# Token attention: queries and keys from one projection of 128 columns, parts put in place by transfers inside SBUF

## The chip, the cores and the metric

One core of a Trainium2 chip runs the whole program. The metric is device time in microseconds; before the change the median of three runs is 577.97 us (576.04 to 580.85).

## The reference, cut to what matters

The input is x, four images of 128 channels and 32 x 32 pixels. A convolution attention is added to it, then a token attention, then a mixture of eight experts of which each token takes two. The change touches the token attention alone, for each image with 1024 tokens of 128 channels:

```python
def _L1_attn_ref(inputs, W_q, W_k, W_v, W_o, b_o):
    Q = jnp.einsum('bsd,du->bsu', inputs, W_q)
    K = jnp.einsum('bsd,du->bsu', inputs, W_k)
    V = jnp.einsum('bsd,du->bsu', inputs, W_v)
    attn = jnp.einsum('bqu,bku->bqk', Q, K) * scale
    w = jax.nn.softmax(attn, axis=-1)
    out = jnp.einsum('bqk,bku->bqu', w, V)
    return jnp.einsum('bsu,ud->bsd', out, W_o) + b_o + inputs
```

Here d is 128 and u is 64; inputs are the tokens after a layer norm.

## The kernel before

The attention part is a run of eight phases: convolution phases of images 0, 1 and 2, token phase of image 0, convolution phase of image 3, token phases of images 1, 2 and 3. Each phase has eight steps, one for each tile of 128 queries. The steps are pipelined: in step g TensorE computes the scores of step g + 1 into one of two score buffers S, transposes the probabilities of step g (L1244), and multiplies those of step g - 1 with the values (L1258, L1264). VectorE takes the row minimum of the (negated) scores (L885) and in convolution phases copies half of the transposed probabilities (L894); ScalarE does the exponentials (L692, L697) and the other copies of probabilities (L706) and outputs (L711).

The preparation of later phases is cut into small units, called fillers, each with a short name, that are spread over three slots in every step. All engines walk the same list: `fill(u, b)` on an engine does that engine's part of unit u of image b. A table of strings sets the order. EARLY normalises an image after its convolution attention and before its token attention, MID projects it for the token attention, POST normalises it afterwards. MID is laid over the first slots of a phase, and EARLY or POST of another image over the same slots, one slot later:

```python
SLOTS_OF_STEP = 3
EARLY = "cs0 - - cs1 - ca0 - ca1 c0 c1 o0 o1 - ts0 - ts1 - ta0 - ta1"
MID = "l0 l1 v0 v1 q0 k0 k1 q1"
POST = "ps0 - - ps1 - pa0 - pa1+pc r0 r1 g0 g1"
```

MID of images 0, 1, 2 and 3 lies in convolution phase 2, convolution phase 3, token phase 1 and token phase 2. In a name, 0 and 1 are the halves of 512 tokens. l transposes the normalised tokens into operandT; v, q and k project values, queries and keys; cs, ps are statistics for a norm (L931, L934, then an inverse square root on GpSimd, L612 and L614); ca, pa apply it (L946); pc copies the normalised tokens to the rows for dispatch (L778). Units with a matmul take the PSUM banks TA and TB by turns, and a unit waits until the one two before it is copied out.

On each engine the three slots of a step stand at fixed places. TensorE: scores, output projection, slot 0, transposes, slot 1, values, slot 2. VectorE: minimum of the next step, normalisation of an output, slot 0, copy of probabilities, slot 1, slot 2. ScalarE: slot 0, copy of probabilities, slot 1, copy of outputs, exponentials of the next step, slot 2.

Scores are computed exactly enough by splitting queries and keys into a rounded part (hi, in the type F32R) and a remainder (lo). QS holds the query's hi in partitions 0 to 63 and its lo in 64 to 127; KH holds the key's hi twice, KL the key's lo twice. Two matmuls, QS with KH and QS with KL, give all four products. Because each tile needs both halves, the weights Wq2 and Wk2 hold W_q and W_k twice, side by side, and a query or key unit projects the same 64 columns into both halves of the partitions. A query unit is one matmul on TensorE (L1358, two passes in the trace), a rounding copy on ScalarE to all of QS (L765) and a subtraction on VectorE for the lower half of QS (L994, 64 partitions); a key unit is L1360, L767 and a subtraction of 128 partitions into KL (L996). VectorE waits for ScalarE's copy (hi_done), and the bank is free only after the subtraction.

QS, KH and KL lie in the tile CQ that the convolution phases also use, in the one of its two buffers that is free at the time. SyncE's queue holds all large transfers in program order: inputs, then for each image the stores and loads that put convolution queries and keys in place (L447 to L463), then the rows of the expert stage.

## Time and profile before

| | us |
|---|---|
| median of three runs | 577.97 |
| lowest and highest | 576.04, 580.85 |
| profiled execution, whole | 577.57 |
| its span in the profile | 575.6 |
| attention part, first scores to the first expert tile | about 33 to 363 |
| expert stage | about 363 to 575 |

The profile is one execution. Its span leaves out about 2 us that the device time includes. Busy times of TensorE are modelled at their ends, since matmuls are pipelined: the time at which the next instruction of the queue starts says more than a duration.

### The profile page before, as it was taken

Reading aid. Unit: us, or ns where it says so; the run is one execution under the profiler, and the core shown is the slowest. Engines: PE = TensorE matmul, PEld = TensorE weight load, DVE = VectorE, ACT = ScalarE, POOL = GpSimd, SP = SyncE. Lnnn points to the kernel's source line nnn. Section 1 sums busy time; section 2 is a strip of 40 time slices with the busy share of each in tenths; the row PEclk is TensorE's granted clock in tenths of the full one; section 3 lists DMA queues with packets and bytes.
Section 4 is the critical chain, followed back from the end, with each engine's and each line's share of the span. In section 5 each row is a group of like instructions: output and inputs, shape, how many; then the busy total and the mean of one; then the engine's idle time right before and its main releaser. Section 6 shows DMA issues by size and latency. Waiting matters only on the chain.

```text
span 575.6 us, 11859 instructions
## 1 busy us (share of the span) xinstructions
PE 476.1 (83%) x3510; PEld 372.4 (65%) x3511; DVE 349.9 (61%) x1023; ACT 304.8 (53%) x794; POOL 182.0 (32%) x199
## 2 busy tenths in 40 slices
PE   3758878788688997898998967788988998998891
PEld 3447666566466766676777756467766876876770
DVE  4633686677855767577976758274783443445461
ACT  2237776677665687666566645335533443443341
POOL 4001001131130230010454443167655773333230
PEclk9959999998999998899899979799999999999896
DMA  8595712500005200000000010112222331226424
GB/s 260 146 229 184 204 27 85 145 1 2 2 1 174 56 1 1 2 2 1 6 29 30 24 34 29 47 47 75 72 66 61 93 100 51 60 60 193 143 96 132
DMA packets 39066, 42.74 MB, mean 74 GB/s; under 512 B 6555, under 2 KB 29556, under 8 KB 39012
## 3 DMA queue, kind: packets, MB, share of 16 engines
q1 hardware_dynamic: 33242, 31.94, 20.3%
q0 software_dynamic: 4608, 9.99, 5.1%
q8 instruction: 29, 0.48, 0.4%
q10 hardware_dynamic: 1162, 0.14, 0.2%
q14 instruction: 25, 0.20, 0.1%
HBM read 24.73 MB, written 17.85 MB: 74 GB/s over the span
## 4 chain that ended last, share of the span: by engine, by line
PE 56%; DVE 14%; ACT 11%; issue 10%; DMA 6%; SPq 1%; POOL 1%; DVEq 0%; POOLq 0%; ACTq 0%
PE S L1409 12%; PE S L1244 8%; PE PO L1425 7%; ACT shared L692 6%; PE TA L1417 3%; PE OM L1258 2%; PE S L1236 2%; PE OM L1264 2%; DVE lowest L885 2%; DMA xs<-slots 2%; PE S L1237 2%; DVE late L946 2%; ACT shared L706 2%; PE TA L1340 2%; PE OM L1401 1%
## 5 line engine op out<-in xcount | busy, mean ns | idle before, releaser
L885 DVE TENSOR_REDUCE lowest<-S 128x4 f32<-128x1024 f32 (+1 forms) x64 | 78.0, 1220 | 57.8 <-PE S L1232 30.2
L1409 PE MATMUL S<-w_T,shared 128*128 x284 | 97.0, 465 | 5.5 <-ACT shared L792 4.4
L602 POOL DMA_INDIRECT y_rows<-shared,xs x71 | 68.2, 960 | 89.8 <-ACT shared L803 81.7
L1244 PE MATMUL S<-ident,shared 128*128 128x128 f32 x512 | 73.2, 290 | 17.1 <-ACT shared L692 15.9
L706 ACT ACTIVATE shared<-S 128x512 f32<-128x512 f32 (+1 forms) x64 | 51.8, 809 | 58.7 <-PE S L1244 58.7
L1166 DVE TENSOR_TENSOR late<-S,shared 128x341 f32<-128x341 f32 x71 | 36.4, 513 | 70.6 <-ACT shared L797 70.4
L1244 PEld LDWEIGHTS S<-ident,shared 128*128 128x128 f32 x512 | 61.1, 148 | 27.6 <-ACT shared L692 21.4
L596 POOL DMA_INDIRECT slots<-rows_both,pos_i x64 | 62.4, 975 | 43.0 <-PE S L1244 23.8
L797 ACT ACTIVATE shared<-S 128x341 f32<-128x341 f32 x71 | 32.3, 455 | 81.2 <-PE S L1409 80.1
L1425 PE MATMUL PO<-w_T,shared 114*128 x426 | 61.6, 281 | 10.2 <-DVE shared L1171 5.6
L1425 PEld LDWEIGHTS PO<-w_T,shared 114*128 114x128 f32 x426 | 53.5, 192 | 24.2 <-issue 17.4
L692 ACT ACTIVATE shared<-S,lowest 128x256 f32<-128x256 f32 x128 | 58.7, 478 | 10.7 <-DVE lowest L885 10.7
L1409 PEld LDWEIGHTS S<-w_T,shared 128*128 128x128 f32 x284 | 49.8, 196 | 22.4 <-issue 9.1
L612 POOL TENSOR_SCALAR rs_v<-mv 128x8 f32<-128x8 f32 x12 | 2.9, 243 | 160.8 <-DVE mv L934 160.8
L1171 DVE COPY shared<-TA 114x384 f32<-114x384 f32 x71 | 39.5, 556 | 17.8 <-PE TA L1417 13.8
L803 ACT ACTIVATE shared<-PO,xs 128x128 f32<-128x128 f32 x71 | 26.1, 367 | 27.0 <-PE PO L1425 26.9
L1232 PE MATMUL S<-CK,CQ 96*128 96x256 f32 x128 | 26.9, 337 | 12.4 <-DMA CQ<-q_pass 6.1
L697 ACT ACTIVATE shared<-S,lowest 128x1024 f32<-128x1024 f32 x32 | 35.5, 1111 | 1.8 <-DVE lowest L885 1.6
L1264 PE MATMUL OM<-shared,Vt 128*64 128x128 f32 x512 | 36.1, 284 | 0.0
L1417 PE MATMUL TA<-ident,late 128*114 128x128 f32 x213 | 35.7, 276 | 0.0
L1236 PE MATMUL S<-CQ 128*128 128x512 f32 x64 | 30.0, 468 | 6.2 <-ACT shared L706 3.1
L1264 PEld LDWEIGHTS OM<-shared,Vt 128*64 128x64 f32 x512 | 28.2, 140 | 8.7 <-issue 8.5
(297 smaller groups left out, 839.2 us busy)
## 6 DMA issues: line engine op xcount, KB each, us to landing
CQ<-q_pass SPq DMA_DIRECT2D x24, 256.0 KB, 5.1
xs<-slots SPq DMA_DIRECT2D x71, 65.0 KB, 1.9
late<-y_rows SPq DMA_DIRECT2D x8, 512.0 KB, 4.8
q_pass<-late SPq DMA_DIRECT2D x6, 512.0 KB, 3.6
x<-in_x SPq DMA_DIRECT2D x4, 512.0 KB, 6.0
out<-x SPq DMA_DIRECT2D x8, 256.0 KB, 2.1
CK<-k_pass SPq DMA_DIRECT2D x12, 128.0 KB, 3.0
rows_both<-in_L_ffn_w SPq DMA_DIRECT2D x1, 1364.0 KB, 9.1
```

Of the source, the lines that this page charges most:

```text
L596: pool.indirect_dma_start(slots, bass.IndirectOffsetOnAxis(pos_i[:, b % 2, j % 2, j // 2:j // 2 + 1], 0), rows[j % 2][:, (b % 2) * NT + j ...
L602: pool.indirect_dma_start(y_rows, bass.IndirectOffsetOnAxis(xs[:, k, C:C + 1].bitcast(I32), 0), ys[:, k % NC, :], None).then_inc(ys_out[k] ...
L692: ins = act.activation(probs[:, g % 2, h * KEYS:(h + 1) * KEYS], S[g % 2][:, h * KEYS:(h + 1) * KEYS], ACT.Exp, bias=lowest[:, g % 2, h:h ...
L706: act.activation(probsT[:, g % 2, at:HW], S[g % 2][:, at:HW], ACT.Copy).then_inc(s["ptB_copied"], 1)
L885: nc.vector.tensor_reduce(lowest[:, g % 2, 0:n], S[g % 2][:, :].rearrange("p (h k) -> p h k", h=n), AX.X, ALU.min).then_inc(s["low_ready"], 1)
L1171: nc.vector.tensor_copy(hidT[0:HC, k % NC, :], TA[0:HC, 0:CHUNKS * P]).then_inc(s["hT_dve"], 1)
L1236: mm(dst, QS[T][:, tile(j)], KH[T][:, r], start=True, stop=False)
L1244: last = tr(S[g % 2][:, tile(k)], probs[:, g % 2, tile(k)], ident[:, :])
L1264: last = mm(out_[r, :], Vt[:, b % 2, kt, :], pT[:, tile(kt)], start=(kt < 2), stop=(kt >= NT - 2))
L1409: last = mm(S[k % 2][:, m * 512:m * 512 + H], xsT[:, k % NC, :], w13_T[:, bass.ds(e, 1), m * H:(m + 1) * H].rearrange("p a h -> p (a h)"), ...
L1417: last = tr(TA[0:HC, tile(c)], hid[:, k % NC, c * HC:(c + 1) * HC], ident[:, :])
L1425: last = mm(PO[:, 0:P], hidT[0:HC, k % NC, tile(c)], w2_T[0:HC, bass.ds(e, 1), tile(c)].rearrange("p a c -> p (a c)"), start=(c == 0), sto ...
```

## The change

The weights of queries and keys stand side by side in one tile Wqk, of which the query half is scaled. One unit, m, projects both for half of the tokens: partitions 0 to 63 get queries, 64 to 127 keys. ScalarE's rounding copy writes to QS, so that QS has the query's hi above and the key's hi below; VectorE's subtraction writes both remainders to KL. A new function of SyncE, move_qk, then puts the parts in place by transfers from one part of SBUF to another, with a wait between them: the key's hi from the lower half of QS to both halves of KH; the query's lo from the upper half of KL to the lower half of QS; the key's lo from the lower half of KL to its upper half. The first scores of a token phase wait for all three. MID has six units instead of eight, with m0 and m1 ahead of the values.

```diff
-MID = "l0 l1 v0 v1 q0 k0 k1 q1"
+MID = "l0 l1 m0 m1 v0 v1"
...
-            for dst, w in ((Wq2, "L1_attn_W_q"), (Wk2, "L1_attn_W_k"), (Wv2, "L1_attn_W_v")):
-                for k in range(2):
-                    sp.dma_start(dst[:, k * U:(k + 1) * U], a[w]).then_inc(s["small_in"], 16)
+            for dst, k, w in ((Wqk, 0, "L1_attn_W_q"), (Wqk, 1, "L1_attn_W_k"), (Wv2, 0, "L1_attn_W_v"), (Wv2, 1, "L1_attn_W_v")):
+                sp.dma_start(dst[:, k * U:(k + 1) * U], a[w]).then_inc(s["small_in"], 16)
...
+            def move_qk(b):
+
+                T = TOK_SET[b]
+                wait_copied(sp, ("m0", b), ("m1", b))
+                for k in range(2):
+                    sp.dma_start(KH[T][k * U:(k + 1) * U, :].bitcast(F32), QS[T][U:P, :].bitcast(F32)).then_inc(s["k_moved"], 16)
+                sp.wait_ge(s["k_moved"], 32 * (b + 1))
+                sp.dma_start(QS[T][U:P, :].bitcast(F32), KL[T][0:U, :].bitcast(F32)).then_inc(s["q_moved"], 16)
+                sp.wait_ge(s["q_moved"], 16 * (b + 1))
+                sp.dma_start(KL[T][0:U, :].bitcast(F32), KL[T][U:P, :].bitcast(F32)).then_inc(s["kl_moved"], 16)
...
                 stack_q(b, 1)
+                if b == 2:
+                    move_qk(0)
+            for b in range(1, B):
+                move_qk(b)
...
-                elif u in ("q0", "q1"):
+                elif u in ("m0", "m1"):
                     act.activation(QS[T][:, r], bank[:, :], ACT.Copy).then_inc(s["hi_done"], 1)
-                elif u in ("k0", "k1"):
-                    act.activation(KH[T][:, r], bank[:, :], ACT.Copy).then_inc(s["hi_done"], 1)
...
-                elif u in ("q0", "q1"):
-                    copied(V.tensor_tensor(QS[T][U:P, r], bank[U:P, :], QS[T][U:P, r].bitcast(F32), ALU.subtract))
-                elif u in ("k0", "k1"):
-                    copied(V.tensor_tensor(KL[T][:, r], bank[:, :], KH[T][:, r].bitcast(F32), ALU.subtract))
+                elif u in ("m0", "m1"):
+                    copied(V.tensor_tensor(KL[T][:, r], bank[:, :], QS[T][:, r].bitcast(F32), ALU.subtract))
...
+                    if kind == "tok":
+                        pe.wait_ge(s["k_moved"], 32 * (b + 1))
+                        pe.wait_ge(s["q_moved"], 16 * (b + 1))
+                        pe.wait_ge(s["kl_moved"], 16 * (b + 1))
...
-                elif u in ("q0", "q1"):
+                elif u in ("m0", "m1"):
                     pe.wait_ge(s["wq_scaled"], 1)
-                    last = mm(bank[:, :], Wq2[:, :], operandT[:, r], start=True, stop=True)
-                elif u in ("k0", "k1"):
-                    last = mm(bank[:, :], Wk2[:, :], operandT[:, r], start=True, stop=True)
+                    last = mm(bank[:, :], Wqk[:, :], operandT[:, r], start=True, stop=True)
```

VectorE in the first three steps of convolution phase 2, before, where image 0 is projected. CQ is the tile that holds QS, KH and KL, late the normalised tokens of image 1, shared the transposed probabilities, TA and TB the PSUM banks:

```order
L934 BN_AGGR mv<-stats 128x2 x4
L885 TENSOR_REDUCE lowest<-S 128x4
...
L894 COPY shared<-S 128x512
L994 TENSOR_TENSOR CQ<-TA,CQ 64x512
L931 BN_STATS stats<-late 128x6 x4
L934 BN_AGGR mv<-stats 128x2 x4
L996 TENSOR_TENSOR CQ<-TB,CQ 128x512
L885 TENSOR_REDUCE lowest<-S 128x4
...
L996 TENSOR_TENSOR CQ<-TA,CQ 128x512
L946 TENSOR_SCALAR late<-late,mv,rs_y 128x128 x4
L894 COPY shared<-S 128x512
L994 TENSOR_TENSOR CQ<-TB,CQ 64x512
```

The same stretch now:

```order
L945 BN_AGGR mv<-stats 128x2 x4
L1005 TENSOR_TENSOR CQ<-TA,CQ 128x512
L896 TENSOR_REDUCE lowest<-S 128x4
...
L1005 TENSOR_TENSOR CQ<-TB,CQ 128x512
L905 COPY shared<-S 128x512
L942 BN_STATS stats<-late 128x6 x4
L945 BN_AGGR mv<-stats 128x2 x4
L896 TENSOR_REDUCE lowest<-S 128x4
...
L957 TENSOR_SCALAR late<-late,mv,rs_y 128x128 x4
L905 COPY shared<-S 128x512
```

Four subtractions have become two, and these stand one step earlier, the first ahead of a row minimum and the second ahead of a copy of probabilities.

TensorE in token phase 1, before, where image 2 is projected, from its first unit after the transposes of the tokens to the third step's values. Wv, Wq and Wk are the weights, ident marks a transpose, Vt the values:

```order
L1363 MATMUL TA<-Wv,operandT 128x128 x4
...
L1363 MATMUL TB<-Wv,operandT 128x128 x4
L1244 MATMUL S<-ident,shared 128x128 x8
L1358 MATMUL TA<-operandT,Wq 128x512
L1264 MATMUL OM<-shared,Vt 64x128 x8
L1360 MATMUL TB<-operandT,Wk 128x512
...
L1275 MATMUL PO<-Wo,outT 128x128
L1360 MATMUL TA<-operandT,Wk 128x512
L1244 MATMUL S<-ident,shared 128x128 x8
L1358 MATMUL TB<-operandT,Wq 128x512
L1264 MATMUL OM<-shared,Vt 64x128 x8
```

The same stretch now:

```order
L1371 MATMUL TA<-operandT,Wqk 128x512
...
L1371 MATMUL TB<-operandT,Wqk 128x512
L1257 MATMUL S<-ident,shared 128x128 x8
L1374 MATMUL TA<-Wv,operandT 128x128 x4
L1277 MATMUL OM<-shared,Vt 64x128 x8
L1374 MATMUL TB<-Wv,operandT 128x128 x4
...
L1288 MATMUL PO<-Wo,outT 128x128
L1257 MATMUL S<-ident,shared 128x128 x8
L1277 MATMUL OM<-shared,Vt 64x128 x8
```

The merged units have taken the places of the value units, the value units those of the first query and key unit, and in the third step transposes and values follow each other without a unit between them.

## Rows read from the trace of the kernel before

**Rows 1.** The page's first part: span, then TensorE's busy time, share and instructions.

```profile
span 575.6 us, 11859 instructions
PE 476.1 (83%) x3510; PEld 372.4 (65%) x3511; DVE 349.9 (61%) x1023; ACT 304.8 (53%) x794; POOL 182.0 (32%) x199
```

**Rows 2.** Groups by line and shape: busy us, mean ns of one, idle before.

```profile
L1358 PE MATMUL TA<-operandT,Wq 128*128 128x512 f32 x8 | 4.1, 594 | 0.0
L994 DVE TENSOR_TENSOR CQ<-TA,CQ 64x512 fp32r<-64x512 f32 x4 | 2.8, 694 | 3.4 <-ACT CQ L765 3.4
L765 ACT ACTIVATE CQ<-TA 128x512 fp32r<-128x512 f32 x4 | 2.4, 594 | 0.5 <-PE TA L1358 0.5
```

**Rows 3.** Order of time, convolution phase 2: start us, us, engine, instruction, idle before.

```profile
126.99 0.40 ACT L769 ACTIVATE Vt<-TA 128x256 f32<-128x256 f32 x1
...
130.65 0.87 DVE L931 BATCH_NORM_STATS2 stats<-late 128x6 f32<-128x128 f32 x4
...
131.55 0.38 DVE L934 BATCH_NORM_AGGREGATE mv<-stats 128x2 f32<-128x6 f32 x4
...
132.44 1.67 POOL L614 TENSOR_TENSOR rs_y<-rs_v,minus_half 128x8 f32<-128x8 f32 x1
...
133.12 1.22 DVE L885 TENSOR_REDUCE lowest<-S 128x4 f32<-128x1024 f32 x1
...
134.66 0.68 DVE L996 TENSOR_TENSOR CQ<-TA,CQ 128x512 fp32r<-128x512 f32 x1
...
135.26 1.11 DVE L946 TENSOR_SCALAR late<-late,mv,rs_y 128x128 f32<-128x128 f32 x4
...
136.28 0.69 DVE L894 COPY shared<-S 128x512 f32<-128x512 f32 x1
...
137.00 0.69 DVE L994 TENSOR_TENSOR CQ<-TB,CQ 64x512 fp32r<-64x512 f32 x1
...
137.02 0.74 PE L1232 MATMUL S<-CK,CQ 96*128 96x256 f32 x4 [2.04 <-DVE shared L894]
...
137.72 1.11 DVE L946 TENSOR_SCALAR late<-late,mv,rs_y 128x128 f32<-128x128 f32 x4
...
138.32 1.91 PE L1244 MATMUL S<-ident,shared 128*128 128x128 f32 x8
...
138.87 1.23 DVE L885 TENSOR_REDUCE lowest<-S 128x4 f32<-128x1024 f32 x1
```

**Rows 4.** Windows: us, PE, PEld, DVE, ACT, POOL busy (instructions), PEclk, DMA, GB/s.

```profile
138.00:143.00 5.00, 5.00 (x38) 4.07 (x36) 3.04 (x8) 2.91 (x9) 0.00 (x0) 0.66 0.00 2
240.00:262.00 22.00, 21.79 (x184) 16.57 (x184) 14.32 (x41) 16.58 (x31) 1.90 (x2) 1.00 0.00 1
```

**Rows 5.** Order of time, convolution phase 3.

```profile
219.39 1.11 DVE L946 TENSOR_SCALAR late<-x,mv,rs_y 128x128 f32<-128x128 f32 x4
...
220.60 2.01 ACT L778 ACTIVATE rows_both<-late 128x1024 f32<-128x1024 f32 x2 [1.79 <-DVE late L946]
```

**Rows 6.** Order of time, token phase 1, third step, TensorE.

```profile
252.32 1.02 PE L1360 MATMUL TA<-operandT,Wk 128*128 128x512 f32 x2
...
253.18 1.04 PE L1244 MATMUL S<-ident,shared 128*128 128x128 f32 x8
...
254.06 1.02 PE L1358 MATMUL TB<-operandT,Wq 128*128 128x512 f32 x2
...
255.01 1.09 PE L1264 MATMUL OM<-shared,Vt 128*64 128x128 f32 x16
```

**Rows 7.** Order of time, token phase 2, ScalarE.

```profile
300.15 2.01 ACT L778 ACTIVATE rows_both<-late 128x1024 f32<-128x1024 f32 x2 [0.64 <-DVE late L946]
```

**Rows 8.** DMA issues (KB each, median us to landing), and image 1's first token scores.

```profile
CQ<-q_pass SPq DMA_DIRECT2D x24, 256.0 KB, 5.1
out<-x SPq DMA_DIRECT2D x8, 256.0 KB, 2.1
...
236.97 0.50 PE L1236 MATMUL S<-CQ 128*128 128x512 f32 x1 [0.21 <-DVE shared L894]
```

More of the change, by code:

```diff
@@ L122 @@
     LAST_UNITS
-BANKED = [f for f in FILLERS if f[0] in "kT0 kT1 qv0 qv1 Q0 Q1 K V c0 c1 o0 o1 l0 l1 q0 q1 k0 k1 v0 v1 r0 r1 g0 g1 wa wb wc rank".split()]
+BANKED = [f for f in FILLERS if f[0] in "kT0 kT1 qv0 qv1 Q0 Q1 K V c0 c1 o0 o1 l0 l1 m0 m1 v0 v1 r0 r1 g0 g1 wa wb wc rank".split()]
 NORMS = [f for f in FILLERS if f[0] in ("cs1", "ts1", "ps1")]
@@ L167, in build @@
         o_wTg = sb("o_wTg", [P, P])
-        Wq2 = sb("Wq2", [P, P])
-        Wk2 = sb("Wk2", [P, P])
+        Wqk = sb("Wqk", [P, P])
         Wv2 = sb("Wv2", [P, P])
@@ L271, in build @@
         OM, PO, TA, TB = (ps(n, [P, 512]) for n in ("OM", "PO", "TA", "TB"))
-        names = """wq_scaled x_in0 x_in wKQV_in w_in const_z const_set pad_z wt_done wt_used bias_done bias_used gn_pe gn_dve gn_read w1_in w3_in
+        names = """k_moved q_moved kl_moved wq_scaled x_in0 x_in wKQV_in w_in const_z const_set pad_z wt_done wt_used bias_done bias_used gn_pe gn_dve gn_read w1_in w3_in
             w2stage_in small_in rows_in dve_pre q_put0 q_put1 k_put q_stacked0 q_stacked1 k_stacked scores_done low_ready exp_done pt_done ptA_copied ptB_copied
@@ L642, in step @@
                 slot(2)
-            pool.wait_ge(s["small_in"], 16 * 8)
-            nc.gpsimd.tensor_scalar(Wq2[:, :], Wq2[:, :], -TOK_SCALE, None, ALU.mult).then_inc(s["wq_scaled"], 1)
+            pool.wait_ge(s["small_in"], 16 * 6)
+            nc.gpsimd.tensor_scalar(Wqk[:, 0:U], Wqk[:, 0:U], -TOK_SCALE, None, ALU.mult).then_inc(s["wq_scaled"], 1)
             pool.wait_ge(s["bias_used"], 3)
@@ L952, in fill @@
                 V = nc.vector
-                if u in ("Q0", "Q1", "K", "q0", "q1", "k0", "k1"):
-                    dve.wait_ge(s["hi_done"], sum(g[0] in ("Q0", "Q1", "K", "q0", "q1", "k0", "k1") for g in FILLERS[:FILLERS.index(f) + 1]))
+                if u in ("Q0", "Q1", "K", "m0", "m1"):
+                    dve.wait_ge(s["hi_done"], sum(g[0] in ("Q0", "Q1", "K", "m0", "m1") for g in FILLERS[:FILLERS.index(f) + 1]))
                 elif u in ("V", "wc", "g0", "g1", "re"):
@@ L1223, in scores @@
                         pe.wait_ge(s["q_stacked0"], 16 * 3 * (b + 1))
-                    wait_copied(pe, *((u, b) for u in (("V",) if kind == "conv" else ("q0", "q1", "k0", "k1", "v0", "v1"))))
+                    wait_copied(pe, *((u, b) for u in (("V",) if kind == "conv" else ("m0", "m1", "v0", "v1"))))
+                    if kind == "tok":
+                        pe.wait_ge(s["k_moved"], 32 * (b + 1))
+                        pe.wait_ge(s["q_moved"], 16 * (b + 1))
+                        pe.wait_ge(s["kl_moved"], 16 * (b + 1))
                 if j == NT // 2 and kind == "conv":
@@ L1319, in fill @@
                 for k, sources in {"Q": ("kT",), "K": ("qv0", "qv1"), "V": ("qv0", "qv1"), "o": ("c",),
-                                   "v": ("l",), "q": ("l",) if u[:2] != "qv" else (), "k": ("l",) if u[:2] != "kT" else (),
+                                   "v": ("l",), "m": ("l",),
                                    "g": ("r",)}.items():
@@ L1392, in _ @@
             pe.wait_ge(s["const_set"], 3)
-            pe.wait_ge(s["small_in"], 16 * 8)
+            pe.wait_ge(s["small_in"], 16 * 6)
             pe.wait_ge(s["bias_used"], 3)
```

## The prediction, made before the change was run

> **What bounds the kernel now.** I read the page's first part, then the groups of instructions by line, then the order of time in the four places where a token image is projected, then the DMA issues. The span of 575.6 us has TensorE busy for 83% of it [rows 1]; VectorE and ScalarE are less busy, but the attention stages are a loop in lockstep (scores, row minimum, exponentials, transposes, copy out, values), so what counts is which engine closes the loop in a given step, and that differs between the places. I call them A (image 0, projected inside convolution phase 2, about 122 to 140 us), B (image 1, inside convolution phase 3, the same pattern 81.67 us later: its last normalisation starts at 219.39 against 137.72 in A [rows 3, 5]), C (image 2, inside token phase 1, about 243 to 259 us) and D (image 3, inside token phase 2, about 284 to 302 us).
>
> The work that the change touches is small: 16 copies on ScalarE and 16 subtractions on VectorE of 0.59 to 0.69 us each, four images times four units, and as many projections on TensorE, each a pair of matmul passes of 594 ns [rows 2], where each row is the share of one bank and one kind. Outside the four places the rows of instructions are unchanged.
>
> In A and B, VectorE closes the loop. In the third step of A it runs without a gap: minimum at 133.12, subtraction of a key half at 134.66, first half of the normalisation at 135.26, and only at 136.28 the copy of the probabilities for which TensorE waits: its next scores start at 137.02 after 2.04 us idle. Then the subtraction of a query half at 137.00, the other half of the normalisation at 137.72, and the next minimum at 138.87, although its scores had been there before [rows 3]. In C and D TensorE closes the loop: in 240 to 262 us it is busy 21.79 of 22.00 us [rows 4], and the last two projections stand squarely in its queue, from 252.32 to 253.18 before the transposes and from 254.06 to 255.01 before the values [rows 6].
>
> **The change part by part.** Two projections of an image go, those in the third step. The first two steps keep as many units as before: the two merged projections stand where the two value projections stood, and these where the first query and the first key projection stood; the second key and the second query projection, in the third step, have no successor. On TensorE that is an even trade: a merged unit fills about 0.86 us (252.32 to 253.18), and the value unit that it changes places with was in the same queue before.
>
> TensorE: per image 2 units, 0.86 + 0.95 = 1.81 us; four images 7.2 us. ScalarE: 2 copies of 0.594 us, 1.2 us per image. VectorE: 2 operations of about 0.69 us (the half-height L994 costs as much as a full one), 1.38 us per image. These don't add up, since they lie beside each other; the place decides which counts.
>
> Place A, replayed from rows 3. The value copy at 126.99 becomes the rounding copy of the first merged unit, 0.60 us, to 127.59. Behind it VectorE subtracts (0.69, to 128.3), and only then takes the minimum of that step. Minimum with what follows it to the next own operation is 133.12 to 134.66, 1.54 us: 129.8. Second subtraction 0.69: 130.5. Probability copy, 136.28 to 137.00, 0.72: 131.2. Four statistics and aggregates, 130.65 to 131.93, 1.28: 132.5, where they ended at 131.93. So the early part of the step is later by 0.5 us, and with it GpSimd's square root: it ended at 132.44 + 1.67 = 134.11 and will end at about 134.6. The minimum at 133.12 now follows the statistics directly, 132.4, and ends with its followers at 133.95. The normalisation therefore starts at 134.6 instead of 135.26, and the probability copy comes about 0.7 us earlier, at 135.6. This is the gain of A: 0.7 us, less than the two subtractions, because the square root is late next. The second half of the normalisation then gains another 0.7 to 0.8, which matters only where something waits for it.
>
> Place B: something does. ScalarE copies the rows of image 0 for dispatch there, 2.01 us at 220.60, and waited 1.79 us for exactly that second half [rows 5]. That start moves by about 1.5 us. Behind it TensorE's values and transposes under the lowered clock move by 0.7 only. Between 0.7 and 1.5 I take 1.1 us.
>
> Place C: transposes start 0.86 us earlier, values 1.81 earlier [rows 6]. VectorE has no probability copy there, so the early subtractions delay nothing that is waited for: the minimum moved behind the first subtraction should still be done before the exponentials that want it, since ScalarE reaches them only after its copies. I take 1.7 us. Place D is C with the row copy of ScalarE at 300.15, which waits for the normalisation [rows 7]; that one moves by the two subtractions and more, so TensorE's 1.81 stands: 1.8 us.
>
> Sum: 0.7 + 1.1 + 1.7 + 1.8 = 5.3 us. Each place gives between nothing (a wait elsewhere takes it up) and about 1.95 us (all of VectorE's 1.38 plus the 0.6 by which its minimum starts earlier).
>
> The new transfers: per image two copies of the key half (64 partitions of 4 KB, 256 KB each, side by side), then one of the query remainder, then one of the key remainder, three hops in series on SyncE's queue. The trace has no transfer inside SBUF. The nearest rows of the same size are 2.1 us (SBUF to memory) and 5.1 us (memory into 32 partitions) to landing [rows 8]; I take the slow one, since few partitions is what they have in common: 3 x 5.1 = 15.3 us. In B the second subtraction ends about 130.5 + 81.7 = 212.2 us and the first scores of image 1 are at 236.97 [rows 8], 24.7 us later, so 9 us are left over; A and C have 25 us and more. Cost: nothing by either end. By the Trainium skill, page "SBUF — State Buffer", section on the DMA port swizzle, a transfer on 64 partitions reaches only half of the SBUF ports; an estimate with its 218 GB/s is 1.2 us of pure movement for 256 KB, so it would not fill the slack either. The trace agrees in kind only: 32 partitions took 5.1 us where 128 took 2.1 us [rows 8], with other sources and more packets.
>
> On SyncE nothing waits behind these hops that is needed soon: after image 0's comes the key store of convolution image 3, tens of microseconds later, and after the rest the token loads, which wait for the routing table. TensorE gets three more semaphore waits at the start of each token phase and two fewer copy waits; I count nothing. Two small weight loads at the start go away, nothing on the path.
>
> **The rivals.** First, a larger gain. In A and B the granted clock falls just after TensorE's wait: 0.66 on average in 138 to 143 us, which is between the two levels of 1.2 and 2.4 GHz, and the eight transposes at 138.32 take 1.91 us [rows 3, 4]. If the shorter step avoids that, up to 5.00 x 0.34 = 1.7 us comes back at each of the two places, and with the full 1.95 elsewhere the gain is 8 to 9.5 us: 568.3 to 570 us. Against it: by the replay TensorE's idle time before the scores of A even grows a little (its last projection is gone), so the low stretch should stay. Chance 0.15.
>
> Second, the gain is taken up. The early subtractions put ScalarE's copy, VectorE's subtraction and the minimum in series in the first step; if the delay of 0.5 us passes through to the exponentials, A and B give nothing and C and D 1 us each: 576 us. For it speaks that in B and D ScalarE carries a 2 us copy at the same spot; against it the 0.86 and 0.95 us blocks in a full TensorE queue. Chance 0.24.
>
> Third, slower through the clock. Less matmul work between waits may lower the clock at places where it is full now. Each new low stretch costs up to the same 1.7 us; it decides from the fourth on: 572.5 + 4 x 1.7 = 579.3 us, 1.3 above the median before. By the Trainium skill, page "TensorE: Matmul & The Clock Gate", Part 1, the chip sets this clock by how busy the array has been lately, so by that rule removing projections can cost what it saves; the trace agrees that the low stretch follows an idle wait (2.04 us [rows 3]) and shows a full clock, 1.00, in 240 to 262 us where the queue is full [rows 4], and it stays nearly full there without the two units. Chance 0.06.
>
> Fourth, slower through the hops. Were a hop longer than 24.7 / 3 = 8.2 us, each token phase would begin late: at 12 us a hop, 36 - 24.7 = 11 us a phase, four times, 45 us less the 5.3, some 617 us. No row comes near. Chance 0.04. The forecast itself holds 0.51.
>
> **How the numbers follow.** The profiled execution took 577.57 us (span 575.6), 0.4 under the median of 577.97 of the runs shown. 577.57 - 5.3 = 572.3; from the median 572.7; I say 572.5. The range: down to 568.2 for the larger gain, up to 577.3 where nearly all is taken up; it leaves out the two slower rivals and the ends. About 1% (5.8 us, 572.2) is what a measurement of this kernel can tell from no change, and the forecast lies just inside: of its 0.51, 0.27 falls beyond 1%. With the larger gain, 0.15, faster by over 1% has 0.42; within 1% has 0.24 + 0.24 + most of the third rival, 0.06 less 0.01: 0.53; slower by over 1% the rest, 0.05.
>
> **What would show it.** Right: in A the probability copy of the third step about 0.7 us earlier relative to the first step, with the normalisation waiting for GpSimd; in C transposes directly behind the output projection and the values 1.8 us earlier; each hop landing in 2 to 5 us, and no wait at the first scores of a token phase. Wrong: a first step longer by over 0.5 us in C or D, a hop above 8.2 us, or the granted clock below 1.00 in 240 to 262 us. The expert stage behind the attention must keep its length; if it does not, the difference there is not of this change.

## The result and the profile after

Over 20 runs of each kernel on the same chips the changed kernel took 572.95 us (median, 566.85 to 579.95) and the kernel before 579.76 us (574.66 to 584.61, and one run of 2524.37). The ratio is 0.988, with a 95% interval of 0.9858 to 0.9903: 6.8 us faster, where 572.5 us in all and a gain of 5.3 us were forecast. A repeat of the changed kernel in another set gave 573.0 against 579.48 us, ratio 0.9894 (0.9858 to 0.9929). Both kernels have single slow runs, over 1.5% above their fastest; the ratios here and below leave these out, so they are not quite the quotients of the medians.

The page's first part, to set beside [rows 1]:

```profile
span 574.0 us, 11821 instructions
...
PE 475.6 (83%) x3494; PEld 375.2 (65%) x3495; DVE 343.0 (60%) x1015; ACT 301.0 (52%) x786; POOL 182.1 (32%) x199
```

VectorE loses 6.9 us and 8 instructions, ScalarE 3.8 us and 8, which is the count of the change. TensorE loses 16 matmuls but only 0.5 us of busy time. These sums tell little: the same eight transposes take 1.04 us at the full granted clock and 1.91 us at the lower level, and most of the low stretches lie elsewhere in every execution. The span of this one execution is only 1.6 us shorter than before, because its attention began 2.65 us later (first copy of probabilities at 42.45 us, before 39.8) and its stages outside the four places ran 3.1 us longer. So I read place by place.

The measure is ScalarE's copy of probabilities, which comes once in each step. From the copy in an image's first projecting step to the copy four steps later, before the change:

```profile
123.98 0.60 ACT L706 ACTIVATE shared<-S 128x512 f32<-128x512 f32 x1 [0.69 <-PE S L1244]
...
146.05 0.60 ACT L706 ACTIVATE shared<-S 128x512 f32<-128x512 f32 x1 [0.18 <-PE S L1244]
...
205.08 0.60 ACT L706 ACTIVATE shared<-S 128x512 f32<-128x512 f32 x1 [0.69 <-PE S L1244]
...
227.23 0.60 ACT L706 ACTIVATE shared<-S 128x512 f32<-128x512 f32 x1 [1.19 <-PE S L1244]
...
243.53 1.02 ACT L706 ACTIVATE shared<-S 128x1024 f32<-128x1024 f32 x1 [0.28 <-PE S L1244]
...
265.03 1.02 ACT L706 ACTIVATE shared<-S 128x1024 f32<-128x1024 f32 x1 [0.18 <-PE S L1244]
...
284.95 1.02 ACT L706 ACTIVATE shared<-S 128x1024 f32<-128x1024 f32 x1 [0.29 <-PE S L1244]
...
306.89 1.02 ACT L706 ACTIVATE shared<-S 128x1024 f32<-128x1024 f32 x1 [1.58 <-PE S L1244]
```

and the same copies after it:

```profile
126.69 0.60 ACT L719 ACTIVATE shared<-S 128x512 f32<-128x512 f32 x1 [0.69 <-PE S L1257]
...
146.37 0.60 ACT L719 ACTIVATE shared<-S 128x512 f32<-128x512 f32 x1 [0.18 <-PE S L1257]
...
206.08 0.60 ACT L719 ACTIVATE shared<-S 128x512 f32<-128x512 f32 x1 [0.69 <-PE S L1257]
...
227.12 0.60 ACT L719 ACTIVATE shared<-S 128x512 f32<-128x512 f32 x1 [1.32 <-PE S L1257]
...
242.21 1.02 ACT L719 ACTIVATE shared<-S 128x1024 f32<-128x1024 f32 x1 [0.28 <-PE S L1257]
...
262.23 1.02 ACT L719 ACTIVATE shared<-S 128x1024 f32<-128x1024 f32 x1 [0.18 <-PE S L1257]
...
282.34 1.02 ACT L719 ACTIVATE shared<-S 128x1024 f32<-128x1024 f32 x1 [0.28 <-PE S L1257]
...
302.23 1.02 ACT L719 ACTIVATE shared<-S 128x1024 f32<-128x1024 f32 x1 [1.58 <-PE S L1257]
```

The differences of each pair are the first two lines of this table; the others are worked out in the same way from the other runs' traces (us):

```
                                   A      B      C      D     sum
before                          22.07  22.15  21.50  21.94   87.66
changed                         19.68  21.04  20.02  19.89   80.63
before, repeated                22.09  22.17  21.50  21.95   87.71
changed, repeated               19.67  20.94  20.00  19.89   80.50
changed, TensorE work back      20.09  20.70  21.52  21.31   83.62
changed, VectorE work back      21.22  21.03  20.24  21.08   83.57
changed, both back              20.10  21.04  21.50  21.30   83.94
changed, all three back         20.10  21.04  21.49  21.30   83.93
before, units in new order      20.74  21.49  21.50  21.30   85.03
changed, values first           19.86  21.27  19.99  20.45   81.57
changed, normalisation later    18.67  19.85  20.00  19.90   78.42
before, normalisation later     22.29  22.16  21.97  22.54   88.96
changed, 5 hops                 21.28  21.02  19.98  19.88   82.16
changed, 15 hops                21.24  20.98  20.00  19.90   82.12
```

The repeats agree within 0.1 us, far better than whole runs do (they spread by 10 us). But A depends on more than the kernel. It is 19.7 us in both traces of the changed kernel itself and 21.2 to 21.3 us in those with longer hops, by the clock, as will be seen. The four places give 2.4, 1.1, 1.5 and 2.05 us: 7.0 us, against 6.8 measured.

Place A of the changed kernel in order of time, to set beside [rows 3]:

```profile
130.35 0.69 DVE L1005 TENSOR_TENSOR CQ<-TA,CQ 128x512 fp32r<-128x512 f32 x1 [1.78 <-ACT CQ L778]
...
132.50 0.68 DVE L1005 TENSOR_TENSOR CQ<-TB,CQ 128x512 fp32r<-128x512 f32 x1
...
133.10 0.68 DVE L905 COPY shared<-S 128x512 f32<-128x512 f32 x1
...
135.48 1.67 POOL L627 TENSOR_TENSOR rs_y<-rs_v,minus_half 128x8 f32<-128x8 f32 x1
...
137.19 1.12 DVE L957 TENSOR_SCALAR late<-late,mv,rs_y 128x128 f32<-128x128 f32 x4 [0.58 <-POOL rs_y L627]
...
138.22 0.68 DVE L905 COPY shared<-S 128x512 f32<-128x512 f32 x1
...
138.96 0.74 PE L1245 MATMUL S<-CK,CQ 96*128 96x256 f32 x4 [2.17 <-DVE shared L905]
...
140.08 1.04 PE L1257 MATMUL S<-ident,shared 128*128 128x128 f32 x8
```

The normalisation now waits 0.58 us for GpSimd's square root. The probability copy of the third step comes 138.22 - 126.69 = 11.53 us after that of the first; before it was 136.28 - 123.98 = 12.30. That is 0.77 us. TensorE's wait before the scores is no shorter (2.17 us, 2.04 in [rows 3]), yet the transposes behind it take 1.04 us instead of 1.91. The window says why; its columns are those of [rows 4]:

```profile
138.00:143.00 5.00, 4.04 (x43) 3.44 (x44) 4.03 (x11) 3.40 (x12) 0.00 (x0) 1.00 0.47 107
```

The granted clock is 1.00 where it was 0.66 at the same spot before. In the repeat of before it was low there again (0.69), in the repeat of the changed kernel full again. But the step alone does not settle it: with five hops instead of three, and the same rows up to here, the same wait of 2.17 us was followed by

```profile
138.89 1.91 PE L1258 MATMUL S<-ident,shared 128*128 128x128 f32 x8
```

and A took 21.28 us, 0.8 less than before instead of 2.4. Split at the third step's copy on VectorE, A falls into few values. Behind that copy lie 8.15 to 8.16 us where the granted clock is full (changed kernel, its repeat, the values first, the kernel before in the new order) and 9.76 to 9.78 where it is low (before, its repeat, five hops). So before to changed, 0.77 us of the 2.39 lie ahead of the copy, and the other 1.62 are the clock's.

Place C of the changed kernel, TensorE, beside [rows 6]:

```profile
250.81 0.38 PE L1288 MATMUL PO<-Wo,outT 128*128 128x128 f32 x2
251.03 1.04 PE L1257 MATMUL S<-ident,shared 128*128 128x128 f32 x8
252.00 1.09 PE L1277 MATMUL OM<-shared,Vt 128*64 128x128 f32 x16
```

Output projection, transposes and values follow each other, with no projection of query or key between them. And the hops, in the DMA issues (KB each, median us to landing), beside [rows 8]:

```profile
CQ<-CQ SPq DMA_DIRECT2D x16, 256.0 KB, 3.0
```

A hop takes 3.0 us (2.8 to 4.2), not 5.1. No engine waits for one. From the last probability copy to the end, the span took 575.6 - 360.01 = 215.6 us before and 574.0 - 358.72 = 215.3 after: the expert stage kept its length.

B and D have one more row that counts, ScalarE's copy of the normalised rows, which waits for VectorE's second half of the normalisation. In B and in D of the changed kernel, beside [rows 5] and [rows 7]:

```profile
219.89 2.01 ACT L789 ACTIVATE rows_both<-late 128x1024 f32<-128x1024 f32 x2 [1.11 <-DVE late L957]
...
295.50 2.01 ACT L789 ACTIVATE rows_both<-late 128x1024 f32<-128x1024 f32 x2 [0.32 <-DVE late L957]
```

Counted from the first copy of probabilities it starts at 13.81 us in B (before 15.52) and at 13.16 in D (before 15.20), 1.7 and 2.0 us earlier. In D the copy that ends the place comes 6.73 us behind it, before 6.74. In B that distance was 6.63 and is 7.23 now: the low clock (transposes of 1.91 us) keeps back 0.6 of the 1.7 us.

### The profile page after: what moved, and what is told of

It is laid out like the page before. It is cut to its first block, busy times and chain, and to the rows that moved or that the text cites. A ratio compares the mean times of both kernels' runs of the same rounds, so it can differ in the third digit from the quotient of the medians.

```text
span 574.0 us, 11821 instructions
## 1 busy us (share of the span) xinstructions
PE 475.6 (83%) x3494; PEld 375.2 (65%) x3495; DVE 343.0 (60%) x1015; ACT 301.0 (52%) x786; POOL 182.1 (32%) x199
## 3 DMA queue, kind: packets, MB, share of 16 engines
q0 software_dynamic: 4608, 9.99, 5.2%
## 4 chain that ended last, share of the span: by engine, by line
PE 52%; DVE 13%; ACT 11%; issue 9%; DMA 7%; POOL 4%; SPq 1%; DVEq 0%; POOLq 0%; ACTq 0%
PE S L1420 9%; PE S L1257 9%; ACT shared L705 6%; PE PO L1436 6%; PE S L1249 3%; PE OM L1277 3%; DMA xs<-slots 2%; PE TA L1428 2%; PE OM L1271 2%; ACT shared L719 2%; PE S L1250 2%; PE TA L1353 2%; DVE lowest L896 2%; POOL slots L609 2%; POOL y_rows L615 2%
## 5 line engine op out<-in xcount | busy, mean ns | idle before, releaser
L814 ACT ACTIVATE shared<-PO,xs 128x128 f32<-128x128 f32 x71 | 26.1, 368 | 26.7 <-PE PO L1436 26.6
```

## The experiments

They ran in three sets, each beside runs of the kernel before in the same set (medians 579.48, 580.58 and 579.18 us).

**The repeats.** The changed kernel unchanged, and the kernel before unchanged, as a measure of what repeats.

> The changed kernel again, as the reference point of this set. Theory: about 1.2% under the kernel before (some 7 us). In its profile the gain from the copy of probabilities of the first projecting step to that of the fifth is 1.5 us in place A without a low stretch of the clock, 1.1 in B, 1.5 in C, 2.0 in D. Rival (the gain is a matter of where the clock falls): these four differences scatter by more than a microsecond against the first profile.

> The kernel before once more, for a second profile of it. If the low stretch of the clock in place A belongs to the kernel before, place A (copy of probabilities of the first to the fifth projecting step) again takes about 22 us with transposes of 1.9 us in it, and B 22; if it fell there by chance, A takes about 20.5 us, and 1.5 us of what A gained in the first pair of profiles was chance. The time is that of the kernel before, within 0.3%.

Measured: 573.0 us, ratio 0.9894 (0.9858 to 0.9929), and 580.11 us, ratio 1.0026 (0.9982 to 1.0071). The low stretches at 138 and at 220 us came back in the repeat of before; most other low stretches lie elsewhere each time.

**TensorE's removed work put back.** Unused matmuls of the same size in the third step; their result is read by nothing.

```
-MID = "l0 l1 m0 m1 v0 v1"
+MID = "l0 l1 m0 m1 v0 v1 d0 d1"
 ...
+                if u in ("d0", "d1"):
+                    g = ("v" + u[1], b)
+                    wait_copied(pe, g)
+                    nc.tensor.matmul(BANKS[bank_of(g)][:, :], Wqk[:, :], operandT[:, int(u[1]) * 512:int(u[1]) * 512 + 512], start=True, stop=True)
```

> Two projections of 128x512 per image put back in the third step on TensorE alone; their result is not used. Theory (TensorE closes the loop in C and D): it takes back 1.5 us in C and 1.8 in D, at most 0.8 in each of A and B; 3.5 to 5 us slower than the changed kernel. Rival (the removed subtractions are what counted): no difference.

Measured: 574.94 us, ratio 0.9928 (0.9898 to 0.9959). C and D are longer by 1.5 and 1.4 us, A by 0.4, and B is shorter by 0.2 to 0.3. So what the change saves on TensorE counts in C and D and hardly in A and B. In B the extra work fills the wait in front of the scores:

```profile
218.55 0.74 PE L1245 MATMUL S<-CK,CQ 96*128 96x256 f32 x4 [0.74 <-DVE shared L905]
...
220.03 1.10 PE L1257 MATMUL S<-ident,shared 128*128 128x128 f32 x8 [0.20 <-ACT shared L705]
```

against the changed kernel itself:

```profile
218.82 0.97 PE L1245 MATMUL S<-CK,CQ 96*128 96x256 f32 x4 [2.21 <-DVE shared L905]
...
220.66 1.91 PE L1257 MATMUL S<-ident,shared 128*128 128x128 f32 x8
```

The wait falls from 2.21 to 0.74 us and the transposes run at the full clock, 1.10 us instead of 1.91. Removing TensorE's work there saves nothing in these traces. The clock is full there in all three traces with unused matmuls, but in the next experiment it is full without them as well, so that they kept it up is likely and not shown.

**VectorE's removed work put back.** An unused subtraction of constants in each of the two units, into a scratch tile.

```
+                elif u in ("d0", "d1"):
+                    w_ = wQV_T[:, :, :, :].rearrange("p a m c -> p (a m c)")
+                    wait_if(dve, s["scratch_set"], before_it(f, "d0", "d1"))
+                    V.tensor_tensor(scratch[:, 0:512], w_[:, 0:512], w_[:, 512:1024], ALU.subtract).then_inc(s["scratch_set"], 1)
```

> Two subtractions of 128x512 (0.69 us each) per image put back in the third step on VectorE alone, on constant data; their result is not used. Theory: in A the first one fills the 0.58 us that VectorE waits for the square root, so A loses 0.1 us, C nothing, B 0.8 and D up to 1.4, because there ScalarE's row copy waits for the second half of the normalisation; 1 to 2.5 us slower than the changed kernel. Rival (VectorE is the bound in all four): 1.4 us in each, 5.5 in all.

Measured: 569.83 us, ratio 0.9863 (0.9821 to 0.9905), from 7 runs that reach from 568.76 to 578.44; its profile is of the 578.44. The interval overlaps that of the repeat (0.9894), so no cost can be told from the times. In the places B is unchanged (21.03), C 0.2 and D 1.2 longer; A is 1.5 longer, but the granted clock is low there in this trace, at 141 us, as in the five-hop run without this work (21.28), so A shows no cost of it. I had B and A down as VectorE's places. That B is unchanged is not proof against it, since this trace has the full clock in B where the changed kernel has the low one:

```profile
220.18 0.74 PE L1250 MATMUL S<-CK,CQ 96*128 96x256 f32 x4 [2.22 <-DVE shared L906]
...
221.31 1.04 PE L1262 MATMUL S<-ident,shared 128*128 128x128 f32 x8
```

ScalarE's row copy starts at 14.40 us, 0.6 later than in the changed kernel, and the place ends 6.63 behind it. So VectorE's work costs 0.6 us of the row copy's start, which the clock gave back here.

**Both put back.** The two edits together.

> Both of the above together, results not used. Theory: the two overlap, so it is 5 to 6.5 us slower than the changed kernel, that is within 0.2% of the kernel before. Rival (part of the gain lies outside the third steps, for example in the two weight loads that are gone at the start): it stays 2 us or more faster than the kernel before.

Measured: 575.91 us, ratio 0.9949 (0.9912 to 0.9986), still 3.6 us faster than before, and the places still 3.7 us shorter. Something other than this work gives half of the gain in the places.

**All three put back.** ScalarE gets its copies back too, into scratch that nothing reads.

```
+                elif u in ("d0", "d1"):
+                    wait_if(act, s["scratch_a_set"], before_it(f, "d0", "d1"))
+                    act.activation(scratch_a[:, :], operandT[:, r], ACT.Copy).then_inc(s["scratch_a_set"], 1)
```

> The changed kernel with unused work of the removed kind put back in the third step on all three engines: a projection on TensorE, a subtraction on VectorE and a copy on ScalarE for each of two units. Theory: what the change gains is the removed work plus the earlier place of the subtractions; with all of it back, D returns to 21.9 and C to 21.5, B comes to 21.6 (0.5 more than with two engines put back), and A keeps 1.3 from the order of its subtractions: about 577 us, ratio 0.995 to 1.00. Rival: ScalarE's copies are covered wherever they stand, and the places stay as with two engines put back (A 20.1, B 21.0, C 21.5, D 21.3): ratio 0.995 or less.

Measured: 575.85 us, ratio 0.9938 (0.9901 to 0.9975). The rival holds: no place moves by more than 0.01 us against the run with two engines put back. ScalarE's copies were free. The removed instructions together are worth 83.93 - 80.63 = 3.3 us by the places, 2.2 us by the times (575.85 against the changed kernel with five hops, 573.66, in the same set). The other 87.66 - 83.93 = 3.7 us stay. Where a part of them comes from is seen in B, where this run has as many VectorE operations as the kernel before. Before, VectorE's waits in B's second step, and its third step:

```profile
211.58 0.69 DVE L994 TENSOR_TENSOR CQ<-TA,CQ 64x512 fp32r<-64x512 f32 x1 [0.80 <-ACT CQ L765]
...
214.18 0.69 DVE L996 TENSOR_TENSOR CQ<-TB,CQ 128x512 fp32r<-128x512 f32 x1 [0.58 <-ACT CQ L767]
...
216.92 1.11 DVE L946 TENSOR_SCALAR late<-x,mv,rs_y 128x128 f32<-128x128 f32 x4
217.95 0.68 DVE L894 COPY shared<-S 128x512 f32<-128x512 f32 x1
```

With all three put back:

```profile
209.71 0.69 DVE L1010 TENSOR_TENSOR CQ<-TA,CQ 128x512 fp32r<-128x512 f32 x1 [2.21 <-ACT CQ L780]
...
211.90 0.68 DVE L1010 TENSOR_TENSOR CQ<-TB,CQ 128x512 fp32r<-128x512 f32 x1
...
215.93 0.68 DVE L1014 TENSOR_TENSOR scratch<-wQV_T 128x512 bf16<-128x512 f32 x1
216.59 1.11 DVE L962 TENSOR_SCALAR late<-x,mv,rs_y 128x128 f32<-128x128 f32 x4
217.62 0.68 DVE L910 COPY shared<-S 128x512 f32<-128x512 f32 x1
...
220.02 2.01 ACT L794 ACTIVATE rows_both<-late 128x1024 f32<-128x1024 f32 x2 [0.23 <-DVE late L962]
```

Counted from the first step's copy (205.08 and 205.62), the third one comes at 12.87 before and at 12.00 here, 0.87 earlier with the same number of operations, and at 12.01 in the changed kernel (218.09 - 206.08). Before, two subtractions in mid-step made VectorE wait 0.80 and 0.58 us for ScalarE's rounding copies. In the new order it waits once, 2.21 us, in the step where it had little to do, and the extra subtraction of the third step fills the time in which the normalisation would wait for the square root. The row copy starts at 14.40 us instead of 15.52, and behind it lie 6.64 us, before 6.63: that is all of B's 1.11. So in B, with the number of operations as before, the earlier place of the subtractions gives the gain. One limit: the unused work waits for no other engine, as the real work did.

D's 0.64 us have the same source. The row copy starts at 14.44 us (297.54 - 283.10), with no wait, instead of 15.20 after a wait of 0.64 for VectorE; behind it lie 6.86 us, before 6.74. In A the third copy is 0.77 earlier, and behind it lie 8.57 us: 1.20 less than before, which is the clock's 1.62 less 0.42 for TensorE's work. So of the 3.7 us that stay some 2.5 are order (0.77, 1.11 and 0.64) and 1.2 the clock's.

**The kernel before with its units in the new order.** The same idea from the other side, all real work kept.

```
-MID = "l0 l1 v0 v1 q0 k0 k1 q1"
+MID = "l0 l1 q0 k0 k1 q1 v0 v1"
```

> The kernel before with all its eight units, in the order l0 l1 q0 k0 k1 q1 v0 v1: the same work, with the values and not the projections in the third step, so that VectorE has no subtraction there. Theory (in A and B VectorE's place in the third step counts, in C and D the amount in TensorE's queue): A and B as much shorter as in the changed kernel, C and D unchanged; 2 to 4 us faster than before. Rival (only the amount of work counts): no difference from before.

Measured: 578.77 us, ratio 0.9987 (0.9934 to 1.004). The places shorten by 2.6 us (A 1.3, B 0.7, C 0, D 0.6), but the time cannot be told from before, nor from a gain of 2.6 us, which its interval holds. In the trace the attention as a whole is no shorter (361.11 - 40.59 = 320.5 us, before 320.2). What the places gain is lost to the clock in phases that the edit does not touch: the last three steps of convolution phase 1 are 1.4 us longer, at a granted clock of 0.50 to 0.84, and the first step of token phase 0 is 1.5 us longer, at 0.70, as it also is in the trace with both put back (0.71). Nor is A's 1.3 us order: the third copy comes at 12.58 us, 0.28 later than before, and the clock is full. With all four real subtractions ahead of the third step nothing is gained there. In B and D the row copy does start earlier, by 0.66 and 0.75 us.

**The values first in the changed kernel**, so that the merged units stand where query and key stood.

```
-MID = "l0 l1 m0 m1 v0 v1"
+MID = "l0 l1 v0 v1 m0 m1"
```

> The changed kernel with the values ahead of the merged units (l0 l1 v0 v1 m0 m1), so that the subtractions stand in the second step as before, and the transfers start a step later. Theory: in A the statistics are no longer delayed by a subtraction ahead of them but by the one waiting for ScalarE, as before the change; A and B within 0.5 us of the changed kernel, C and D equal; the same time within 0.3%. Rival (the early subtractions cost the changed kernel the 0.5 us that was predicted in each place): 1 to 2 us faster than the changed kernel.

Measured: 572.31 us, ratio 0.9906 (0.9854 to 0.9958), as the changed kernel. The places sum to 0.9 us more, which a time cannot show. The order among the four units matters little once all of them fit in two steps.

**The normalisation one slot later.** If it waits for the square root and holds up the probability copy, it should stand behind that copy.

```
-EARLY = "cs0 - - cs1 - ca0 - ca1 c0 c1 o0 o1 - ts0 - ts1 - ta0 - ta1"
+EARLY = "cs0 - - cs1 - - ca0 ca1 c0 c1 o0 o1 - ts0 - ts1 - ta0 - ta1"
-POST = "ps0 - - ps1 - pa0 - pa1+pc r0 r1 g0 g1"
+POST = "ps0 - - ps1 - - pa0 pa1+pc r0 r1 g0 g1"
```

> The changed kernel with the first half of each normalisation (ca0, pa0) one slot later, behind VectorE's copy of probabilities in the third step. Theory: in A VectorE no longer waits for the square root before that copy, so the copy comes 1.5 us earlier and TensorE's idle time of 2.2 us before the next scores shrinks to below 1 us; A gives another 1 to 1.5 us, B 0 to 1, the phases with the same pattern (convolution phase 1) 0.5 to 1 us; 2 to 4 us faster than the changed kernel. Rival (the normalised tokens come late for the transposes of the fourth step, which wait in TensorE's queue ahead of the probabilities): no gain or a loss of up to 3 us, above all in C and D.

Measured: 568.19 us, ratio 0.9835 (0.9768 to 0.9903), the lowest median here. A and B are 1.0 and 1.2 us shorter than in the changed kernel, C and D the same. Place A:

```profile
137.76 0.68 DVE L905 COPY shared<-S 128x512 f32<-128x512 f32 x1
138.42 2.14 DVE L957 TENSOR_SCALAR late<-late,mv,rs_y 128x128 f32<-128x128 f32 x8
...
138.50 0.73 PE L1245 MATMUL S<-CK,CQ 96*128 96x256 f32 x4 [0.47 <-DVE shared L905]
```

The copy is out before the normalisation, and TensorE waits 0.47 instead of 2.17 us. The places explain 2.2 us; the medians differ by 4.8 (another set) or 4.1 (the values-first kernel, same set), with 6 runs here and intervals that overlap, so the size beyond 2.2 us stays open.

**The same slot in the kernel before.**

> The kernel before with the first half of the normalisation one slot later, as in the variant of the changed kernel that took 568.2 us. Theory: VectorE closes the loop in A and B of the kernel before just as much, so the probability copy comes out ahead of the normalisation there and A and B shorten by 1 us each (A 21 us, B 21.1), C and D stay at 21.5 and 21.9: 577 us, ratio 0.995 to 0.997. Rival: the slot pays only where the subtractions of the third step are gone, since otherwise they stand in its place on VectorE: no change, ratio 1.00.

Measured: 578.17 us, ratio 0.9984 (0.9959 to 1.0009): the rival holds. In A the copy does come 1.0 us earlier (136.79 - 125.50 = 11.29 against 12.30), and TensorE's wait for it halves. But the other half only moves: TensorE now waits 1.02 us for the normalised tokens, 2.04 in all as before, and the clock falls again:

```profile
137.53 0.74 PE L1232 MATMUL S<-CK,CQ 96*128 96x256 f32 x4 [1.02 <-DVE shared L894]
138.23 2.14 DVE L946 TENSOR_SCALAR late<-late,mv,rs_y 128x128 f32<-128x128 f32 x8
...
139.40 0.71 PE L1351 MATMUL TA<-ident,late 128*128 128x128 f32 x4 [1.02 <-DVE late L946]
...
139.90 1.91 PE L1244 MATMUL S<-ident,shared 128*128 128x128 f32 x8
```

The subtraction of the third step and both halves of the normalisation now stand in a row before the next minimum, and C and D grow by 0.5 and 0.6 us. In B the copy is 1.0 us earlier too and the clock full (transposes of 1.04 us), yet the row copy starts at 15.52 us as before, and B keeps its 22.16. Of these two kernels the slot pays only in the one whose third step is empty.

**Hops lengthened.** The first hop repeated, three and thirteen times in series; the data are the same each time.

```
+                for r_ in range(3):
                     for k in range(2):
                         sp.dma_start(KH[T][k * U:(k + 1) * U, :].bitcast(F32), QS[T][U:P, :].bitcast(F32)).then_inc(s["k_moved"], 16)
-                sp.wait_ge(s["k_moved"], 32 * (b + 1))
+                    sp.wait_ge(s["k_moved"], 32 * (3 * b + r_ + 1))
```

> The first hop of each image is done three times in series: five hops instead of three. With 4.1 us from one first hop to the next (issue, landing 3.3, wait) the chain is 3 x 4.1 + 2.85 + 3.3 = 18.5 us where it was 10.3. In the repeat of the changed kernel the first scores of the following token phase come 22.7 us after the first hop is issued in A (155.19 - 132.51), 22.7 in B (234.30 - 211.65), 18.6 in C (265.88 - 247.31) and only 14.9 in D (302.2 - 287.34). Theory: the chain has room in A and B, just fits in C, and in D delays the last token phase by 3.6 us: a wait of TensorE for the moved parts of about 3.6 us there and the whole 2 to 4 us longer, 575 to 577 us. Rival (the prediction's 24.7 us and more for each place): nothing waits, 573 us.

Measured: 573.66 us, ratio 0.9909 (0.9871 to 0.9946), no wait for a hop anywhere. My expectation was wrong and its rival right: for C and D I had read a later step of the running phase as the start of the next. Image 2's own scores begin at 273.45 us and image 3's at 310.63 (repeat of the changed kernel), so the room is 26.1 and 23.3 us. In A and B it is 23.2 each, counted from the first transfer of the pair (131.96 and 211.14); I had counted from the second. (A is 1.6 us longer in this trace through the clock, as shown above. The first chain ended at 147.67 + 2.8 = 150.5 us, before the phase that needs it, at about 156.9.)

> The first hop thirteen times in series: 13 x 4.1 + 2.85 + 3.3 = 59.5 us. Theory: each token phase begins late by what exceeds its room: 36.8 us in A, 36.8 in B, 40.9 in C, 44.6 in D, 159 us together, so about 571 + 159 = 730 us, with TensorE waiting for the moved parts at the start of each token phase. Rival: other work of the phase is pulled into the wait, or the hops of one image overlap the phase before it, and the total grows by less than 120 us.

Measured: 719.76 us in one run. The first scores of token phases 0 and 2:

```profile
192.20 0.77 PE L1250 MATMUL S<-CQ 128*128 128x512 f32 x1 [37.05 <-DMA CQ<-CQ]
...
382.36 0.77 PE L1250 MATMUL S<-CQ 128*128 128x512 f32 x1 [35.21 <-DMA CQ<-CQ]
```

With 37.12 and 37.44 us in the other two, the four waits sum to 146.8 us, and the time exceeds that of the changed kernel, 573.0, by 146.8 as well: beyond the room every microsecond of a hop is paid in full, in each image, as far as this one run shows. In the first image the chain took 60 us (132.16 to 192.2), so the room is 60 - 37 = 23 us, of which the three hops need 10 to 11.

## Why the prediction came out right, and where it did not

- **The sum.** 5.3 us forecast, 6.8 measured, 7.0 in the places. That the time was met within 0.5 us is luck: the gain was 1.5 us larger, and the profiled execution of before, 577.57 us, from which the time was reckoned, was 2 us under the later median of 579.76. Of the 7.0 us in the places 3.3 are removed work, 2.5 order and 1.2 the clock; the forecast reckoned it as removed work.
- **Place A, 0.7 us.** The replay's 0.7 came out as 0.77, with the wait for the square root that it named (0.58 us). What failed is its account of the cause: "less than the two subtractions" took the gain for removed work, but with all of it put back the copy still comes at 11.53 us (136.89 - 125.36). The early place of the two merged subtractions gives it, and only with two: with the four real ones ahead it came at 12.58. A gave 2.4 us in both traces of the changed kernel, where the granted clock no longer fell at 138 us, and 0.8 us with longer hops, where it did: the 1.6 us between them are the clock's, close to the 1.7 us that the larger-gain rival priced.
- **Place B, 1.1 us.** Size and path were right: the row copy starts 1.7 us earlier (forecast 1.5), and the low clock, which the forecast kept, holds back 0.6 of it. What was wrong is the source: with the removed work put back the row copy is still 1.1 us earlier, by order, and B keeps its 1.1 us, since the clock was full in that trace. With work removed and a full clock B would be about 13.8 + 6.6 = 20.4 us, an estimate from these rows.
- **Place C, 1.7 us.** Measured 1.5, and 1.5 goes when TensorE's work is put back. Here mechanism and size hold.
- **Place D, 1.8 us.** Measured 2.05, but not by TensorE's queue alone. The row copy, which waits for VectorE before (0.64 us) and after (0.32), starts 2.04 us earlier. VectorE's work put back alone costs 1.2 us, TensorE's alone 1.4, all of it 1.4: each engine would have held D back by itself. The other 0.6 is order.
- **The larger gain (0.15).** Its clock half came true in A in both traces of the changed kernel, and not in B. The argument against it, that the low stretch stays because TensorE's wait does not shrink, was the wrong step: the wait was 2.17 us each time, and the clock was full in both traces of the changed kernel and fell in three of its variants (five hops, fifteen hops, VectorE's work back). Its price of 1.7 us holds in A only; in B the clock costs 0.6, since the row copy comes next. By the Trainium skill, page "TensorE: Matmul & The Clock Gate", Part 1, the clock follows how busy the array has been; the run with TensorE's work put back agrees in B (full clock, 1.10 us for the transposes), though the run with VectorE's work back had the full clock there without it.
- **Gain taken up (0.24).** The early delay was there but smaller than 0.5 us: ScalarE's third copy in A comes 9.56 us after the first, before 9.27, and in B 9.99 against 9.83; the next step takes it back and more (14.46 against 16.28 and 16.53 against 17.90). C and D show none (9.89 against 10.73, 10.43 against 11.29).
- **Slower by the clock (0.06).** Not seen in the time. The changed kernel has low stretches elsewhere, but most of them move from run to run.
- **Slower by the hops (0.04).** A hop took 3.0 us, not 5.1. The rule that a hop beyond the room costs in full was right, 146.8 us of it. The statement "A and C have 25 us and more" was right for C (26.1) and too high for A (23.2 in the repeat), and D, which it passed over, has 23.3.

Open: what makes the clock fall in A in one trace and not in another, and how often it does over many runs, so that 1.6 of the 7.0 us may be chance. Open too is whether the kernel before gains in time from the new order; the interval holds both nothing and the 2.6 us of its places.

## What to carry to other kernels

When an edit both removes instructions and moves others forward, put the removed work back as unused work, engine by engine, and read the stage's length in the trace: here half of the gain in the places was not the removed work, and the share of one engine was nothing. Before a stage that did not move is called free of a cost, look whether its clock is the same in both traces. Take the steps' distances from the trace rather than whole times when terms are below 2 us, since they repeated within 0.1 us where times spread by 10, once the granted clock of the stretch is the same. An operation that waits for another engine belongs in the step in which its own engine waits anyway; after such a move look again at what stands in front of the released copy, for the largest further step, 2.2 us in the places, was one slot in a table.

## What was not expected of the hardware

- With unused matmuls on TensorE place B was shorter, 20.70 against 20.94 to 21.04 us, and its granted clock full.
- The granted clock fell after TensorE waits of 2.04 us, in A and B of both traces of the kernel before. It did not after waits of 0.47 to 0.74, nor after 1.56 (the kernel before in the new order). After two waits of 1.02 us (the kernel before with the later slot), after one of 2.17 to 2.22 and after 2.71 (values first) it fell in one place or trace and not in another, with transposes of up to 1.91 and of 1.04 us: the last wait alone does not decide it.
- In B of the kernel before the low clock costs nothing: with the later slot it was full there and the place was 22.16 us, against 22.15.
- A transfer inside SBUF between halves of 64 partitions (256 KB) lands after 2.8 to 4.2 us in the changed kernel's trace, two side by side after 2.9 to 3.8; the next one starts 4.3 us after the pair and 2.9 us after a single one (133.25, 137.51 and 140.36 us in A).
